# Feed-forward layer one of a mixture-of-experts block, computed in pairs of chunks with their last pass in the two halves of the array's rows

## The reference

```
flat = layernorm(h).reshape(512, 192)
probs = softmax(flat @ router_w.T);  top_w, top_i = top_k(probs, 2), normalised
for e in range(8):
    w_e = sum(top_w * (top_i == e))
    hid = gelu(flat @ w1[e] + b1[e])          # 192 -> 768
    out = out + w_e * (hid @ w2[e] + b2[e])   # 768 -> 192
h = h + out
```

## Time and profile before

| | |
|---|---|
| median of 3 runs | 236.63 us (236.3 to 238.28) |
| the profiled execution | 236.4 us, span of its instructions 234.7 us |
| PE busy | 207.4 us, 1162 matmuls |
| DVE, ACT, POOL busy | 139.0, 114.0, 78.0 us |
| granted TensorE clock, mean | 0.905 of full speed |

### The profile page before, as it was taken

The page is one execution under the profiler, slowest core; times in us unless marked ns, Lnnn a source line. Parts: engine busy times, 40 slices in busy tenths (PEclk is TensorE's granted clock), DMA queues, the critical chain, the costliest instruction groups (busy, mean ns, idle before and its releaser), DMA issues.

```text
span 234.7 us, 3493 instructions
## 1 busy us (share of the span) xinstructions
PE 207.4 (88%) x1162; PEld 186.4 (79%) x1162; DVE 139.0 (59%) x306; ACT 114.0 (49%) x199; POOL 78.0 (33%) x90
## 2 busy tenths in 40 slices
PE   0994999998939999595895999999999999999992
PEld 0994999997938886284784989998998999899882
DVE  4499508303693457955399365666467566646654
ACT  2378100107013321222795386786968678694620
POOL 8770000004724003601085144463435446342000
PEclk9997555999976999657999799999999999999999
DMA  6999990000170000000001601607043160000002
GB/s 146 271 328 266 239 188 0 0 3 0 45 190 4 0 0 0 3 0 1 0 0 45 193 0 48 186 0 218 16 124 110 46 189 0 3 0 0 1 3 68
DMA packets 13932, 17.22 MB, mean 73 GB/s; under 512 B 2304, under 2 KB 10113, under 8 KB 13919
## 3 DMA queue, kind: packets, MB, share of 16 engines
q1 hardware_dynamic: 13374, 17.02, 27.1%
q10 hardware_dynamic: 544, 0.03, 0.2%
HBM read 16.66 MB, written 0.39 MB: 73 GB/s over the span
## 4 chain that ended last, share of the span: by engine, by line
PE 76%; DVE 13%; issue 3%; ACT 3%; DMA 2%; POOL 1%; DVEq 0%; ACTq 0%; POOLq 0%
PE ps L357 28%; PE ps L1032 14%; PE ps L1034 6%; PE ps L790 5%; PE ps L804 4%; DMA gb_nat<-in_L_tok_ln_beta 2%; DVE oh L1098 2%; PE ps L741 2%; PE ps L778 2%; DVE big_r L1098 2%; PE ps L875 1%; PE ps L807 1%; PE ps L770 1%; ACT big_r L318 1%; PE ps L919 1%
## 5 line engine op out<-in xcount | busy, mean ns | idle before, releaser
L357 PE MATMUL ps<-big_r,wsplit 128*128 128x512 f32 (+1 forms) x250 | 64.6, 395 | 0.0
L1032 PE MATMUL ps<-wsplit,big_r 128*128 128x384 f32 x192 | 57.6, 359 | 2.8 <-DVE big_r L1098 2.8
L1098 DVE TENSOR_TENSOR big_r<-early,big_r 128x512 fp32r<-128x512 f32 x48 | 43.8, 918 | 26.3 <-ACT big_r L318 25.4
L357 PEld LDWEIGHTS ps<-big_r,wsplit 128*128 128x128 f32 x250 | 44.2, 195 | 6.8
L1034 PE MATMUL ps<-wsplit,big_r 128*128 128x192 f32 x192 | 48.3, 252 | 0.0
L695 ACT ACTIVATE early<-ps,b1t 128x512 f32<-128x512 f32 x48 | 32.8, 682 | 29.4 <-PE ps L357 29.3
L1032 PEld LDWEIGHTS ps<-wsplit,big_r 128*128 128x128 f32 x192 | 36.5, 190 | 5.1 <-DVE big_r L1098 3.2
L1034 PEld LDWEIGHTS ps<-wsplit,big_r 128*128 128x128 f32 x192 | 37.0, 193 | 1.5
L318 ACT ACTIVATE big_r<-early 128x512 fp32r<-128x512 f32 x48 | 30.5, 635 | 1.5
L304 POOL TENSOR_TENSOR wsplit<-stage,wsplit 128x768 fp32r<-128x768 f32 x4 | 7.4, 1849 | 53.4 <-ACT wsplit L318 53.4
L1450 DVE SCALAR_TENSOR_TENSOR t_a<-ps,gates,merge 128x192 f32<-128x192 f32 x32 | 11.8, 411 | 14.8 <-PE ps L1034 14.8
(11 more groups left out here) (214 smaller groups left out, 310.1 us busy)
## 6 DMA issues: line engine op xcount, KB each, us to landing
stage<-in_L_ffn_w SPq DMA_DIRECT2D x4, 576.0 KB, 5.6
early<-in_L_ffn_w SPq DMA_DIRECT2D x4, 576.0 KB, 5.8
shifted<-in_L_tok_w SPq DMA_DIRECT2D x6, 288.0 KB, 8.5
early<-in_x SPq DMA_DIRECT2D x3, 512.0 KB, 6.5
stage<-in_L_ffn_w SPq DMA_DIRECT2D x4, 384.0 KB, 3.4
stage<-in_L_ffn_w SPq DMA_DIRECT2D x8, 192.0 KB, 4.4
early<-in_L_ffn_w SPq DMA_DIRECT2D x4, 384.0 KB, 3.3
early<-in_L_ffn_w SPq DMA_DIRECT2D x8, 192.0 KB, 4.3
```

The lines of the kernel that those rows point to most:

```text
L357: mm = nc.tensor.matmul(dst, lhs, rhs, start=(n == 0), stop=(n == 4))
L1032: nc.tensor.matmul(ps[:, AB[t], 0:2 * D], g_hi[:, j % NG, tok], w2c, start=(f == 0), stop=False)
L1098: return nc.vector.tensor_tensor(o, a, b, op)
```

## The change

Layer one is issued for two chunks at once by a new function, `two_chunks`. It makes four full passes for each chunk, the first four of before. The fifth pass keeps only the product that counts, low by high over 64 features, so that it needs 64 rows of the array: for the even chunk in rows 0 to 63, for the odd one in rows 64 to 127. For that the odd chunks of `W1R` now hold the low part in partitions 0 to 63 and the high part in 64 to 127, and POOL makes the low parts of `W1R` in two operations instead of one. `s_mm1` is raised by 2 after the pair. PE's order is now two chunks of layer one, then two of layer two; in the early part group 1's tokens are transposed after both chunks of group 0. The gates are transposed after chunk 9's layer two, and the gated biases stand between the last two layer twos. ACT's and DVE's orders are as before.

```
-            nc.gpsimd.tensor_tensor(ws[REM:P, W1R:W1R + F], st[REM:P, F:2 * F],
-                                    ws[REM:P, W1R:W1R + F].bitcast(F32), ALU.subtract).then_inc(s_w1lo, 1)
+            nc.gpsimd.tensor_tensor(ws_rest[REM:P, :, 0], st_rest[REM:P, :, 0], ws_rest[REM:P, :, 0].bitcast(F32),
+                                    ALU.subtract).then_inc(s_w1m, 1)
+            pool.wait_ge(s_w1m, e * 2 + 2)
+            nc.gpsimd.tensor_tensor(ws_rest[0:REM, :, 1], st_rest[0:REM, :, 1], ws_rest[0:REM, :, 1].bitcast(F32),
+                                    ALU.subtract).then_inc(s_w1lo, 1)
...
+            def two_chunks(slot, j, cols):
+                ws = wsplit[slot]
+                f0 = j % FC * P
+                for n in range(2):
+                    c0 = f0 + n * P
+                    for k, (a, b) in enumerate(((0, 0), (1, 0), (0, 1), (2, 2))):
+                        nc.tensor.matmul(ps[:, HPB[(j + n) % 4], cols], ws[:, offs[b] + c0:offs[b] + c0 + P],
+                                         n2t[:, a, cols], start=(k == 0), stop=False)
+                for n, rows in enumerate((slice(0, REM), slice(REM, P))):
+                    c0 = f0 + n * P
+                    mm = nc.tensor.matmul(ps[:, HPB[(j + n) % 4], cols], ws[rows, W1R + c0:W1R + c0 + P],
+                                          n2t[rows, 3, cols], start=False, stop=True)
+                return mm
...
-                for j in range(EARLY):
-                    if (g, j) == (0, 1):
-
-                        transposes(1, n2, s_n, lambda t: TT + t + 1, N2B, s_n2t, s_ndup)
-                    mm = triple(ps[:, HPB[j], cols], lambda a: n2t[:, a, cols],
-                                lambda b: wsplit[0][:, offs[b] + j * P:offs[b] + (j + 1) * P], False)
-                    if g == 1:
-                        mm.then_inc(s_mm1, 1)
+                mm = two_chunks(0, 0, cols)
+                if g == 0:
+                    transposes(1, n2, s_n, lambda t: TT + t + 1, N2B, s_n2t, s_ndup)
+                else:
+                    mm.then_inc(s_mm1, 2)
...
-            layer1(0, 2)
...
             def steps(i, last):
-                for j in range(2 * FC):
-                    if j % FC == FC - 1:
-                        layer2(i, j)
-                    if j + LAG < 2 * FC:
-                        layer1(i, j + LAG)
+                for j in range(0, 2 * FC, 2):
+                    if j + 2 < 2 * FC:
+                        layer1(i, j + 2)
                     elif not last:
-                        layer1(i + 1, j + LAG - 2 * FC)
-                    if j % FC < FC - 1:
-                        layer2(i, j)
+                        layer1(i + 1, 0)
+                    layer2(i, j)
+                    if last and j == 2 * FC - 2:
+                        pe.wait_ge(s_gt, 1)
+                        gated_biases()
+                    layer2(i, j + 1)
+                    if last and j == 2 * FC - 4:
...
```

More of the change, by code:

```diff
@@ L265, in vit_tower @@
         HPB = [0, 1, 2, 3]
-        GTB = HPB[(2 * FC - LAG - 1) % 4]
+        GTB = 0
         AB = [4, 5, 6, 7]
@@ L305, in split_low @@
                                     ALU.subtract).then_inc(s_w1m, 1)
-            pool.wait_ge(s_w1m, e + 1)
+            st_rest = st[:, F:2 * F].rearrange("p (c o n) -> p c o n", o=2, n=P)
+            ws_rest = ws[:, W1R:W1R + F].rearrange("p (c o n) -> p c o n", o=2, n=P)
+            pool.wait_ge(s_w1m, e * 2 + 1)
             pool.wait_ge(s_w1hi, e * 2 + 2)
-            nc.gpsimd.tensor_tensor(ws[REM:P, W1R:W1R + F], st[REM:P, F:2 * F],
-                                    ws[REM:P, W1R:W1R + F].bitcast(F32), ALU.subtract).then_inc(s_w1lo, 1)
+            nc.gpsimd.tensor_tensor(ws_rest[REM:P, :, 0], st_rest[REM:P, :, 0], ws_rest[REM:P, :, 0].bitcast(F32),
[3 more added lines that the diff above has]
+                                    ALU.subtract).then_inc(s_w1lo, 1)
             pool.wait_ge(s_w1lo, e + 1)
@@ L1006, in _ @@
             offs = (W1H, W1L, W1R)
+            def two_chunks(slot, j, cols):
[11 more added lines that the diff above has]
+                return mm
             def layer1(i, j):
-                ws = wsplit[j // FC]
-                c0 = (j % FC) * P
                 if j % FC == 0:
-                    pe.wait_ge(s_w1m, i * 2 + j // FC + 1)
+                    pe.wait_ge(s_w1m, (i * 2 + j // FC) * 2 + 2)
                     pe.wait_ge(s_w1lo, i * 2 + j // FC + 1)
-                triple(ps[:, HPB[j % 4], :], lambda a: n2t[:, a, :],
-                       lambda b: ws[:, offs[b] + c0:offs[b] + c0 + P], False).then_inc(s_mm1, 1)
+                two_chunks(j // FC, j, slice(0, T)).then_inc(s_mm1, 2)
             def layer2(i, j):
@@ L1035, in layer2 @@
                                      start=False, stop=(f == FC - 1)).then_inc(s_mm2, 1)
-            pe.wait_ge(s_w1m, 1)
+            pe.wait_ge(s_w1m, 2)
             pe.wait_ge(s_w1lo, 1)
@@ L1068, in steps @@
             def steps(i, last):
-                for j in range(2 * FC):
-                    if j % FC == FC - 1:
-                        layer2(i, j)
-                    if j + LAG < 2 * FC:
-                        layer1(i, j + LAG)
-                    elif not last:
-                        layer1(i + 1, j + LAG - 2 * FC)
-                    if j % FC < FC - 1:
-                        layer2(i, j)
-                    if last and j == 2 * FC - LAG - 1:
+                for j in range(0, 2 * FC, 2):
+                    if j + 2 < 2 * FC:
+                        layer1(i, j + 2)
+                    elif not last:
+                        layer1(i + 1, 0)
[5 more added lines that the diff above has]
+                    if last and j == 2 * FC - 4:
                         pe.wait_ge(s_gate, 1)
                         for t in range(TT):
-                            mm = nc.tensor.transpose(ps[0:E, HPB[j % 4], t * P:(t + 1) * P], gates[:, t], ident)
+                            mm = nc.tensor.transpose(ps[0:E, GTB, t * P:(t + 1) * P], gates[:, t], ident)
                         mm.then_inc(s_gtps, 1)
-                    if last and j == 2 * FC - LAG:
-                        pe.wait_ge(s_gt, 1)
-                        gated_biases()
             with pe.Fori(0, E // 2 - 1) as i:
```

## The result

The changed kernel takes 244.63 us (median of 4 runs, 242.9 to 245.58), the kernel before 237.45 us in the runs beside it: a ratio of 1.029, 95% interval 1.025 to 1.034. It is slower, as forecast, and 1.4 us above the predicted 243.2; the difference is 7.2 us where 6.6 was forecast.

The account below looks back on a forecast made before the run. PE was taken to bound the kernel. From 236.4 us: +5.5 trips, +1.3 boundaries, -0.6 early part, +0.1 POOL, +0.3 tail gave 243.0 profiled, 243.2 us as median; range 236.5 to 246.5.

Parts of the forecast that it names:

- The trip: Layer one on PE: changing to the half tile and back makes each pair 0.26 us longer, +5.5 us over 21 pairs.
- the 0.72: PE time in us of the two half passes with both tile changes, replacing two full passes of 0.457.
- the odd half must load its weights after the even half's, 0.11 us: Inside a pair's half passes on PE: the two weight loads follow one another, adding 0.11 us.
- An expert lasts 14.7 us.: Expert loop: 13.71 before, plus three pairs at 0.26 and one boundary wait of 0.21 us.
- The boundary wait: Expert boundary: PE waits 0.21 us for DVE's low part of chunk 1, held by POOL; six boundaries, +1.3 us.
- The early part: Before PE resumes at chunk 3's layer two: gate products escape POOL's L314, so gates come 0.6 us earlier, -0.6 us.
- Rival 4: Early part: L314 catches the gate products again, or PE's clock drops; 2.6 us more, 245.6 us; chance 0.10.
- POOL's split in two: POOL's low parts of W1R: two operations replace one, between -0.1 and +0.2, taken as +0.1 us once.
- The tail: End of the last expert: PE waits 0.45 us before the gated biases, and layer two 11 ends later, +0.3 us.
- 1: Rival on the half passes: the halves do not run together, +0.40 us a pair, 244.6 to 245 us; chance 0.15.
- 2: Rival: tile change free and halves overlap, but DVE's low parts come late; 236.7 us, no change; chance 0.13.
- 3: Rival: tile change free, halves overlap and DVE is never late; faster, 231.4 us; chance 0.07.

Follow-up runs that it names:

- e2: Changed kernel with both half passes in the same rows, 0 to 63, of the array; 245.68 us in one run.
- e3: Changed kernel with each chunk's half pass right behind its own four full passes, two trips to a pair; 261.4 us in one run.
- e1: Changed kernel with the fifth pass over all 128 rows again, keeping the order of pairs; 243.69 us, ratio 1.024 to the kernel before.
- e4: Changed kernel without any fifth pass (low by high of the last 64 features left out); 237.1 us, ratio 0.994 to the kernel before.
- e7: Changed kernel with a full 128-row fifth pass and POOL's next-expert weight split held until chunk 1's low part is done; 240.36 us, ratio 1.013.
- e10: Changed kernel with the old early order, POOL's first subtraction behind chunk 1's low part, expert 1's second weights behind chunk 5's; half tiles kept; 239.42 us, ratio 1.002.
- e5: Changed kernel with the first two chunks of expert 0 back in the old single-chunk order, group 1's transposes between them; 238.74 us in one run.
- e9: Kernel before, with only POOL's subtraction of expert 1's second weights held until DVE has made chunk 5's low part; 233.7 us, ratio 0.982.
- e11: Same as e10 but with the fifth pass over all 128 rows; 236.27 us, ratio 0.993 to the kernel before.
- e8: Kernel before, with POOL's whole weight split of expert 1 held until the gate values are ready; 236.68 us, ratio 0.995.

## Why the prediction was right, and where it was not

**Sign and size.** Slower was given 0.80, and 244.63 lies in the range. But that the sum came so near was luck: the trips were put 1.9 us too high, the early part 3.0 too low.

**The trip, forecast +0.26 a pair.** Measured 0.17, and 0.157 without waits; for 21 trips 3.6 or 3.3 us instead of 5.5. The mechanism was right: a change costs on the way in and on the way out, and these cost more than the saved pass. One term of the 0.72 failed: "the odd half must load its weights after the even half's, 0.11 us". Both loads run side by side (e2), and two half passes take the 0.43 of one (e3). The Trainium skill says so (TensorE: Matmul & The Clock Gate, Part 3, The mechanism): loads for other rows of the array go on beside running work. The trace agrees, with 0.19 us for two loads against 0.29 in one half; in one half the second load starts beside the first matmul too, 0.10 us later. The ways in and out, put at 0.40 from tiles of 1 and 8 rows, came out at 0.39, which is 0.60 less 0.213 of columns: 0.09 late, 0.22 for one load and the way back together, and 0.08. Only their sum is measured; 0.11 for each of the two in the middle is the prediction's figure for a load and what it leaves. From the start of the eighth full pass to that of layer two there are 0.75 us, where the prediction named 0.95, and the half passes start together and not 0.11 apart.

**"An expert lasts 14.7 us."** It lasts 14.41 = 13.71 + 3 x 0.17 + 0.19.

**The boundary wait, 0.21.** Right, at 0.19, in its place (low part of chunk 1 behind L304) and in its course (it ends 0.54 after POOL). Two errors cancel in it: PE came 0.12 sooner than drawn, by the shorter trip, and POOL and DVE were about as much sooner. Also right was that it grows when pairs get faster: 0.50 in e1, and e4 shows the end of that.

**The early part, -0.6.** This is the step that failed, with +1.39 up to R and 1.23 behind it, of which 0.17 is a trip. The prediction followed L314 and the gate products, and these did escape: the low part of chunk 3 starts 0.98 us earlier behind F, better than forecast. Two things were put at nothing without a reason. The first is what L314 (L319 after) would meet next. That was this low part, which PE waits for: POOL began 0.11 us sooner, and it cost 2.37. The second is what PE had done before it stood still. In the old order, three chunks ahead, it had made the five passes of chunk 6 by then; in pairs they come after R and cost 1.15, as e7 shows without the half tiles. The clock behind the stand was taken as unchanged, and it was, with 3.4 us at 0.50 in both. Rival 4 had the price about right (2.6 above the forecast) with another victim; in e4 its own victim, the gate products, was caught.

**POOL's split in two, +0.1.** Two operations and the gap last 61.40 - 59.22 = 2.18 us, against 1.92 before (57.59 to 59.51): 0.26, above the upper bound of 0.2. Of the 2.1 us ahead of F 1.64 had come before that, as POOL's split itself started that much later (57.32 against 55.68).

**The tail, +0.3.** From layer one of the last expert's third and fourth chunk on PE needs 0.21 us more than before; two trips are 0.34, so the tail as such is 0.1 shorter. PE's wait for the gated biases was about 0.15, not 0.45.

**Rivals.** 1 falls by e2. 2 was wrong in its condition, since the change of tile isn't free, but e4 shows its conclusion: even a free trip would have brought nothing in this order, as PE then waits for DVE's low parts, in the experts and in the early part. 3 needed the boundary waits gone and a trip under 0.457; e10 gave the first and not the second, and ends even with before. 4 is the early part above.

Added up: 3.6 for trips, 1.1 for boundaries (six of 0.19), 2.4 in the early part without its trip, -0.1 in the tail: 7.0 from F to E, where the traces are 6.90 apart. With 0.3 for POOL that is 7.3, and the medians are 7.2 apart; the agreement says little, since the profiled executions are 9.2 apart and 1.64 of that had come before POOL's changed split began. Whether the early part comes out so in every execution was not shown; e2 has the same order ahead of R and needed only 18.58 us for it.

## What to carry to other kernels

Half-height matmuls pay only if what runs inside one change of tile saves more than the change: here 0.60 us a trip against 0.457 for two whole passes, so one saved pass loses and a second would have had to be in the same trip (not tried: it wants the banks of two pairs free at once). Look at which engine feeds the bound one before making it faster: with 11 us of passes taken away, this order was 0.6% faster. Where the bound engine stands still, count what it has already done by then: one chunk less ahead of the stand cost its whole 1.15 us. And where two engines hold each other up, ask of each operation that escapes what is next in line: the cheapest gain here was to hold one POOL operation of 2.7 us behind the work that PE waits for, 3.9 us without any change to PE.

## What the runs showed of the hardware

- A half pass of 512 columns costs 0.43 us to the next full-height instruction, whether one half or both are used (e3, after). The listed 0.50 of each is a modelled end.
- Two loads in different halves fill 0.19 us, two in the same half 0.29 (after, e2).
- A DVE operation of 0.69 us that meets POOL's ends 0.54 us after POOL's. In the early part the one that started first was not held: POOL 0.11 us ahead in after (PE's stand 4.10 us), 0.09 behind in e2 (1.52) and 0.46 behind in e5 (1.16).
- The granted clock stayed at 1.00 behind stands of PE of 0.51 (e9), 1.16 (e5) and 1.52 us (e2), and was 0.50, 1.2 GHz, for 3.4 us at or behind stands of 1.38 (e10), 1.51 (e11), 1.82 (e8), 2.82 (before) and 4.10 us (after). So the length of the stand alone does not decide it. The slow stretch cost 1.6 us (E - R of before and e9) and 1.5 us (after and e5).
